# A three-layer graph network on Trainium2: the last 148 nodes handled as an eleventh pair of 74 and 74

## The reference, cut to what matters

```python
h = jnp.maximum(_layernorm(x, axis=-1), 0.0)          # x: 2708 nodes x 512
def _gc(x, adj, W, b):
    return adj @ (x @ W) + b                          # adj: 2708 x 2708, dense float32
h = relu(_gc(h, adj, W1, b1))                         # 512 -> 1024
h = relu(_gc(h, adj, W2, b2))                         # 1024 -> 1024
return x + _gc(h, adj, W3, b3)                        # 1024 -> 512
```

## Time and profile before

| | |
|---|---|
| median of 3 runs | 1592.84 us (1591.72 to 1594.43) |
| the profiled execution, time | 1593.0 us |
| its span, first to last instruction | 1591.2 us |
| PE busy | 1581.1 us, 7674 matmuls |
| DVE, ACT, POOL busy | 872.1, 610.6, 456.3 us |
| PE clock granted | 1.0 throughout |

### The profile page before, as it was taken

One profiled execution on the slowest core, in us unless ns is written; L12 is line 12 of the kernel. 1 busy time (PEld: TensorE's weight loads), 2 busy tenths in 40 slices (PEclk: granted clock), 3 DMA queues, 4 the chain that ended last, 5 costly groups with the idle time before them and its releaser, 6 DMA issues.

```text
span 1591.2 us, 20930 instructions
## 1 busy us (share of the span) xinstructions
PE 1581.1 (99%) x7674; PEld 1360.1 (85%) x7674; DVE 872.1 (55%) x1361; ACT 610.6 (38%) x1076; POOL 456.3 (29%) x417
## 2 busy tenths in 40 slices
PE   9999999999999999999999999999999999999999
PEld 7788889988889898989898989788898888888898
DVE  8973433256553443434564446564565538766856
ACT  5442222234433332323332333443455536454444
POOL 5863544336654000000000015345402214201302
PEclk9999999999999999999999999999999999999999
DMA  6975657644567554545455658884645336887866
GB/s 244 321 225 205 222 179 220 204 138 152 176 220 235 151 153 143 142 118 148 143 169 161 175 186 282 275 298 133 206 120 133 93 93 202 251 249 220 252 191 198
DMA packets 196628, 303.37 MB, mean 191 GB/s; under 512 B 22632, under 2 KB 92608, under 8 KB 196524
## 3 DMA queue, kind: packets, MB, share of 16 engines
q1 hardware_dynamic: 162268, 223.12, 47.1%
q0 software_dynamic: 12224, 43.16, 8.4%
q10 hardware_dynamic: 22032, 35.74, 6.3%
HBM read 219.44 MB, written 82.50 MB: 190 GB/s over the span
## 4 chain that ended last, share of the span: by engine, by line
PE 91%; DVE 5%; DMA 3%; ACT 1%; issue 0%; ACTq 0%; DVEq 0%
PE ps L1731 30%; PE ps L1733 30%; PE ps L1732 30%; DVE slots L1350 1%; PE ps L1824 1%; DVE still L1332 1%; DMA H<-parts 1%; DVE stats L1279 1%; DMA raw<-adjT 0%; DMA raw<-W 0%; DVE ring L1360 0%; DMA raw<-TS 0%; DMA P<-stage_b 0%; DMA raw<-T 0%; ACT slots L1099 0%
## 5 line engine op out<-in xcount | busy, mean ns | idle before, releaser
L1360 DVE TENSOR_TENSOR ring<-raw,ring 128x512 fp32r<-128x512 f32 (+1 forms) x562 | 404.7, 732 | 426.6 <-ACT ring L1131 424.1
L1131 ACT CAST ring<-raw 128x512 fp32r<-128x512 f32 (+1 forms) x562 | 321.3, 577 | 561.9 <-PE ps L1733 464.8
L1731 PE MATMUL ps<-slots,still 128*128 128x512 f32 (+1 forms) x504 | 183.6, 364 | 2.3 <-DVE slots L1350 1.4
L1733 PE MATMUL ps<-slots,still 128*128 128x512 f32 (+1 forms) x504 | 183.1, 363 | 0.0
L1732 PE MATMUL ps<-slots,still 128*128 128x512 f32 (+1 forms) x504 | 183.1, 363 | 0.0
L1733 PE MATMUL ps<-ring,even 128*128 128x512 f32 (+1 forms) x480 | 174.6, 364 | 0.0
L1732 PE MATMUL ps<-ring,even 128*128 128x512 f32 (+1 forms) x480 | 174.6, 364 | 0.0
L1731 PE MATMUL ps<-ring,even 128*128 128x512 f32 (+1 forms) x480 | 174.6, 364 | 0.0
L1587 POOL DMA_DIRECT2D prep<-P x40 | 26.4, 662 | 465.2 <-DMA P<-U 434.4
L1731 PE MATMUL ps<-ring,S 128*128 128x512 f32 (+1 forms) x420 | 153.0, 364 | 0.6 <-DVE ring L1360 0.6
L1733 PE MATMUL ps<-ring,S 128*128 128x512 f32 (+1 forms) x420 | 152.5, 363 | 0.0
(11 more groups left out here) (162 smaller groups left out, 2891.1 us busy)
## 6 DMA issues: line engine op xcount, KB each, us to landing
raw<-TS SPq DMA_DIRECT2D x160, 256.0 KB, 2.9
raw<-adjT SPq DMA_DIRECT2D x138, 256.0 KB, 3.1
raw<-adjT SPq DMA_DIRECT2D x41, 512.0 KB, 4.6
TS<-made SPq DMA_DIRECT2D x20, 1024.0 KB, 6.6
raw<-TS SPq DMA_DIRECT2D x80, 165.0 KB, 2.4
raw<-HS SPq DMA_DIRECT2D x50, 256.0 KB, 2.7
raw<-P SPq DMA_DIRECT2D x45, 256.0 KB, 4.0
raw<-adjT SPq DMA_DIRECT2D x68, 165.0 KB, 2.6
```

The source lines that it names most:

```text
L1131: act.copy(hi, src).then_inc(hi_done, 1)
L1360: dve.tensor_tensor(lo, src, hi.bitcast(F32), ALU.subtract).then_inc(lo_done, 1)
L1731: pe.matmul(out, st_hi, mv_hi, start=start, stop=False)
L1733: return pe.matmul(out, st_lo, mv_hi, start=False, stop=stop)
```

## The change

Block 20 becomes 74 nodes and block 21 the other 74, and they form an eleventh pair (`EXTRA`) that takes part in all seven products. With 74 rows per block, the three products are 222 rows, which are packed in two operands of 128 rows: the first holds lo (74) and the first 54 rows of hi, against hi and hi; the second holds hi (74) and rows 20 to 73 of hi, against lo, zeros and the last 20 rows of hi. `extra_pair` does two matmuls for each column block and every part. The part `None` goes.

For this each group (part and chunk) now loads: the moving rows once into a raw buffer (74 rows and 54 again), cut by ACT alone; a tail (74 rows and 20 rows); and the stationary rows, from new scratch tensors `HX` (pass 2, two tiles once per part) and `HX3` (pass 3, one tile with four transfers in every group). POOL makes the sums of the extra pair and of its adjacency rows (`prep_extra`, stored in `TX`). `extra2` starts at a multiple of 512 bytes, where `left` did not. In w2 the chunks use e(0..3) and e(4..7) by turns for X and Y (`sides`). At the start, the second half of the first adjacency tile is cut before the scale of the second x tile is worked out. In pass 3 all three adds of x that need part 4 follow part 4.

```diff
+REST = 74
+AGAIN = P - REST
+ONCE = REST - AGAIN
+def sides(chunk):
+    return (0, 4) if chunk % 2 == 0 else (4, 0)
...
+def block_width(block):
+    return P if block < 2 * PAIRS else REST
...
-            for part in (0, 1, 2, 3, None, 4, 5, 6):
+            for part in range(7):
...
+                    if i == 0:
+                        tail_step(g, c)
...
+                    if i == 2:
+                        k = p.tile("extra3", False, 4)
+                        n = 7 * c + part
+                        k.part, k.pair = part, n % 3
+                        k.place_freed = ("group", ends[n - 3] if n > 2 else w3_end)
+                        g.extra = k
+                k = p.tile("left", True, 2, low=False)
...
                 elif j.kind == "left":
-                    sp.dma_start(raw[:, r, 0:WIDTH[j.chunk]], adjT[20 * P:21 * P, columns(j.half, j.chunk)]) \
-                        .then_inc(raw_in[r], 16)
+                    w = WIDTH[j.chunk]
+                    sp.dma_start(raw[0:REST, r, 0:w], extra_rows(j.part, j.chunk, 0, REST)).then_inc(raw_in[r], 16)
+                    sp.dma_start(raw[REST:P, r, 0:w], extra_rows(j.part, j.chunk, 0, AGAIN)).then_inc(raw_in[r], 16)
+                elif j.kind == "extra2":
...
+                    sp.dma_start(raw[0:REST, r, :], src).then_inc(raw_in[r], 16)
+                    sp.dma_start(raw[REST:P, r, :], src[again, :]).then_inc(raw_in[r], 16)
+                elif j.kind == "extra3":
...
+                    src = HX3[EXTRA_PLACE[j.part], :, :]
+                    for half in range(2):
+                        cols = slice(half * QUARTER, (half + 1) * QUARTER)
+                        again = slice(0, AGAIN) if half == 0 else slice(ONCE, REST)
+                        sp.dma_start(raw[0:REST, r, cols], src).then_inc(raw_in[r], 16)
+                        sp.dma_start(raw[REST:P, r, cols], src[again, :]).then_inc(raw_in[r], 16)
...
-                    for r in range(3):
-                        sp.dma_start(raw_tail[r * STEP:r * STEP + TAIL, 0, 0:WIDTH[c]],
-                                     adjT[SHORT * P:N, columns(half, c)]).then_inc(tail_in, 16)
+                    sp.dma_start(raw_tail[0:REST, 0, 0:w], extra_rows(a.part, c, 0, REST)).then_inc(tail_in, 16)
+                    sp.dma_start(raw_tail[REST + AGAIN - ONCE:P, 0, 0:w], extra_rows(a.part, c, AGAIN, REST)) \
+                        .then_inc(tail_in, 16)
...
-            def left_over(g, ms, hi, lo, tail, side, started):
+            def extra_pair(g, ms, first, second):
...
                 for m in range(ms):
...
+                    pe.matmul(out, first[:, cols], ring[:, j.slot % RING, 0, 0:w], start=False, stop=False)
+                    pe.matmul(out, second[:, cols], slot_tails[g.tail[0] % 2][:, 0:w], start=False, stop=True) \
+                        .then_inc(group_done, 1)
```

More of the change, by code:

```diff
@@ L504, in go @@
                 b = g.block
[L505 to L517, removed]
+                if EARLY <= pair_of(b) < PAIRS:
                     buf = ("stash", 2 * (b % PAIRS - EARLY) + b // PAIRS)
@@ L574, in pass3 @@
                 g = p.group("pass3", c, part, [2 * pair, 2 * pair + 1])
-                here = list(ORDER) if part is not None else []
-                half = {1: 0, None: 1, 5: 0, 6: 1}.get(part)
-                for t in here:
+                for i, t in enumerate(ORDER):
                     j = p.tile("moving", True)
@@ L616, in store @@
                 p.steps.append(("store", (g, finals, number)))
-            p.later(4 if part == 1 else 2, store)
+            p.later({1: 4, 4: 9}.get(part, 2), store)
     h1_phase(2)
@@ L874, in gcn_kernel, with kept, sums, rows_of @@
         pass3_groups = [g for g in groups if g.phase == "pass3"]
-        kept = [16 * len([t for t in range(PAIRS) if t % PAIR_BUFS == i]) for i in range(PAIR_BUFS)]
+        extra_turn = BLOCKS.index(20) // 2
+        def kept(i, turns):
+            mine = [t for t in range(turns) if t % PAIR_BUFS == i]
+            return 16 * (len(mine) + (extra_turn in mine))
+        def sums(i):
+            return 32 * len([t for t in range(PAIRS + 1) if t % PAIR_BUFS == i])
+        def rows_of(block):
+            return slice(0, block_width(block))
+        def wait_cut(engine, j):
+            if j.low is None:
+                engine.wait_ge(hi_done, j.cut + 1)
+            else:
+                engine.wait_ge(lo_done, j.low)
         @block.sync
@@ L948, in _, with wait_h1, extra_rows @@
             seen = {"p1": 0, "h2": -1}
+            def wait_h1():
+                seen["h1"] = 1
+                for i in range(PAIR_BUFS):
+                    sp.wait_ge(kept_stored[i], kept(i, PAIRS + 1))
+                    sp.wait_ge(sums_stored[i], sums(i))
+            def extra_rows(part, c, first, last):
+                if part in DIRECT:
+                    k, a = DIRECT[part]
+                    start = 2 * PAIRS * P + k * REST
+                    return adjT[start + first:start + last, columns(a, c)]
+                i = {S2: 3, S3: 1, S1: 0, X22: 2}[part]
+                if ("tx", c) not in seen:
+                    seen["tx", c] = 1
+                    for k in (0, 2):
+                        sp.wait_ge(prep_out[k], 16 * (c + 1))
+                return TX[i, first:last, within(c)]
             def load(j):
```

490 lines of the change are left out of this document (249 added, 241 removed).

## The result

The changed kernel takes **1765.68 us** (median; 1759.39 to 1769.43) against 1592.8: 1.108 times as long, 95% interval 1.104 to 1.112. The profiled execution has a span of 1767.3 us against 1591.2, 176.1 more. The timeline of PE, from each stage's first matmul to the next stage's, says where they lie. "Idle" sums the distances of starts beyond the usual 0.227 or 0.150 us where PE stood; "half clock" is the excess of matmuls that follow at 0.427 or 0.275 us. How the slow matmul right behind a gap is counted moves up to 8 us between these two columns in pass 3 and under 1 us elsewhere; their sum doesn't depend on it.

A forecast was written before the change was run, and what follows sets the result against it. PE, busy 1581.1 of 1591.2 us, bounded the kernel before; in the changed one two DMA engines would bind pass 3. 1593.0 - 7.4 (pass 2) - 1.8 (w2) + 106.7 (pass 3) = 1690.5, forecast 1690 us, range 1640 to 1765.

The forecast's parts named there:

- pass 2: Pass 2: fewer left-over matmuls and an aligned operand save 7.4 us, with the added transfers covered.
- w2: w2, third chunk: X and Y by turns remove PE's wait for ACT's copy, -1.8 us, bounds -1.8 and 0.
- pass 3: Pass 3: waits for transfers make it 381 us in place of 274.3, +106.7; ends 342 and 453.
- pass 1, start: Start: cutting the adjacency half before the second x tile's scale changes 0 us, bounds -0.9 and +0.5.
- PE's own work: Matmuls of passes 2 and 3: PE needs 7.4 us less in pass 2 and 2.4 less in pass 3 (271.9).
- The alignment step: Pass 2: the unaligned left-over operand slows its own and neighbouring matmuls; 2.4 of the 7.4 us depend on it.
- Equal shares, 37 rows for an engine: Transfers of 74 rows: split equally, they run on two engines with 37 rows each; the other bound was 5 rows.
- covered, at the slow price just: Pass 2 transfers: 19.8 to 25.8 us in a wide group's 29, 14.5 to 19.6 in a narrow group's 19.2, so no loss.
- The prediction's last rival: The load binds pass 2 as well: pass 3 at 453, 10 us or more in pass 2, over 1765; chance 0.05.
- Pass 3, groups: Pass 3: two-engine load and five raw buffers make a wide group 20.5 us, a narrow one 15.2, total 393.
- its two prices: Pass 3, rate of one DMA engine: 24.2 GB/s fast; slow 18.6 in wide groups, 18.0 in narrow ones.
- Pass 3, lead of nine tiles, -12 us: Start of pass 3: ring and raw buffers begin nine tiles ahead, saving 12 us, 393 to 381.

The follow-up runs named there:

- 72, 73 and 74 rows: Kernel before, each moving tile of pass 3 loaded as 72 and 56, 73 and 55, or 74 and 54 rows: 1600.4, 2524.9, 2002.1 us.
- 64 + 10 rows: Changed kernel, every transfer of 74 rows (loads and stores) issued as one of 64 and one of 10: 1628.6 us, 1.022 times the kernel before.
- the small parts: Kernel before with aligned left-over operand in pass 2 and X, Y by turns in w2 together: 1588.9 us; with the start order alone: 1593.9 us.

## Why the prediction was right, and where it was not

The sign, the cause and the stage were right: 1690 was forecast, 1765.7 measured, 0.7 us past the upper end of the range (1765). That the range nearly holds the total is luck in part. Pass 3, the stage that the range was drawn for, came out at 424 us, between its ends of 342 and 453, and would alone give 1593.0 - 9.2 + 149.9 = 1733.7; the rest are stalls that the sum had at nothing. By its own steps, spans in us:

| term | forecast | measured |
|---|---|---|
| pass 2 | -7.4 | +15.2 |
| w2 | -1.8 | +7.2 |
| pass 3 | +106.7 | +149.9 |
| pass 1, start | 0 | +3.8 |
| sum | +97.5 | +176.1 |

- **PE's own work**: right. Without idle time and half clock pass 2 is 563.3 - 22.5 = 540.8 us, 7.3 less than before, and pass 3 424.2 - 151.6 = 272.6 against 271.9. The alignment step is shown by the aligned operand alone.
- **Equal shares, 37 rows for an engine**: right in what it makes of the time, by 72, 73 and 74 rows. The sign that the prediction took it from, missing landing times, was weak: in the profile after raw<-TS has none either, with 128 rows a tile (2.9 us before).
- **Pass 2, "covered, at the slow price just"**: the step that failed first. At the slow price its own narrow group wasn't covered (19.6 us in 19.2), but the time was lost elsewhere, in wide groups: it set an average load against an average group. The loads come in bursts, and the first waits for a store of 74 rows that SP, in order, can't pass: SP waits for HX<-pair_buf once, 17.0 us, with three moving tiles issued and all others behind it. With 64 + 10 rows this wait is still 11.9 us, so about 5.1 of the 17.0 are due to two engines; most of the rest is the time until ACT issues the store. SP's wait, and the chain behind:

```profile
SPq L1041 <- DMA HX<-pair_buf: 17.0, 1, 17.0
```

```profile
448.50 0.61 DVE extra L1451
449.12 0.23 SPq L1046
449.39 0.61 SPq L1047
450.04 11.69 DMA raw<-adjT
461.75 0.63 ACT ring L1200
```

  A tile of 128 rows lands after 11.7 us, where 3.1 is the median in the kernel before; by the equal shares a sixteenth of its rows is queued behind shares of 37. Four gaps of 1.7 to 7.5 us in the first chunks of parts 0, 1 and 2, with the half-clock matmuls behind them, make nearly all of the 22.5 us. With 64 + 10 rows they are gone. The prediction's last rival asked for 10 us or more in pass 2 and a total over 1765. Both came, but not its mechanism, groups at the engines' limit throughout.
- **w2**: the wait for ACT's copy is gone, here and with the turns alone, but its 1.8 us was the largest of a wait that comes and goes (see the small parts). Not seen: POOL's sums for w2's moving operands end 30.6 us after w2's start where they ended 21.8 us after it, and PE stood 7.2 us for them. POOL's last four rounds of sums, for these operands, take 68.0 us from their first load on, against 59.6 with 64 + 10 rows, and the gap went there too (w2 203.8 us). POOL's own transfers in these rounds all have 128 rows; which other transfer delays them wasn't taken apart.
- **Pass 3, groups**: 20.5 and 15.2 us forecast, 22.0 and 16.6 measured, 14 x 1.5 + 7 x 1.4 = 31 us. The forecast's 456 KB in 22.0 us would be 20.7 GB/s, its 315 KB in 16.6 us 19.0, between its two prices; how much of a group is the engines' rate and how much the five buffers isn't separated. About 12 of the 31 us can have a cause that was in the diff and that no step named: the store of part 4 that waits for POOL with ACT's casts behind it. It costs 12.3 us in the kernel before; in the changed one, with the transfers slow, it was not measured alone. The prediction looked for waits on PE and SP and let ACT pass as "covered".
- **Pass 3, lead of nine tiles, -12 us**: failed. The forecast 381 us, the groups' 31 and these 12 make the 424. PE used three tiles and then stood 6.5 us for the store and load of the first stationary tile, a stall that the mean of 22.0 us holds.
- **Half clock**: not in the sum at all (last section).
- **Start**: 0 forecast, and 0 shown for the order alone. The 3.8 us after are one gap of 3.0 us at 67.6 and seven matmuls at half clock behind it. Pass 1 takes 310.8 to 312.8 us in all kernels built on the one before, the one with the new order (311.7) among them, and 311.3 to 315.7 in those built on the changed one. DVE is busy nearly all the time there in both; why the gap is longer in some isn't settled.

Of the signs, these held: PE x7638, 0.150 us a matmul in narrow groups, w2's wait gone, DMA share and GB/s down (182 and 153; some 190 forecast), ACT's casts ended by transfers. Pass 2 was 15 us longer and not seven shorter, and pass 3 took 424 us and not some 380.

## What to carry to other kernels

Before a tile gets a new height, factor its number of rows: two pieces of 72 and 56 rows cost 9 us here, 74 and 54 cost 411, 73 and 55 cost 932, with the same bytes; issuing the same 74 rows as 64 and a rest of 10 took back 137 of 173 us. When a change moves an instruction that others wait for (here POOL's final adds), look at every in-order engine that waits for it and at what is queued behind that wait, also on engines far below full. And take a stage's load by its bursts, not by its mean.

## What the runs showed of the hardware that I had not expected

- **Half clock after idle time.** PE's timeline at the start of pass 3 (start us, duration, instruction):

```profile
1343.83 0.39 PE L1828 MATMUL ps<-ring,S 128*128 128x512 f32 x1
1350.74 0.76 PE L1826 MATMUL ps<-ring,S 128*128 128x512 f32 x1 [6.53 <-DVE ring L1451]
1351.31 0.63 PE L1827 MATMUL ps<-ring,S 128*128 128x512 f32 x1
1351.73 0.63 PE L1828 MATMUL ps<-ring,S 128*128 128x512 f32 x1
...
1355.41 0.39 PE L1828 MATMUL ps<-ring,S 128*128 128x512 f32 x1
1355.64 0.40 PE L1826 MATMUL ps<-ring,S 128*128 128x512 f32 x1
```

  Behind 6.5 us of idle time the distance of starts is 0.427 us in place of 0.227, the lower of the two levels (1.2 of 2.4 GHz), for 4.7 us. Over the kernel that is some 40 to 45 us of matmul time; the kernel with 73 rows has a granted clock of 0.60 from 1400 to 1800 us, the one with 72 rows 0.98 from 1400 to 1580. Where PE waits for transfers anyway a slower matmul partly fills time that would be idle, so these can't be added to the transfers' price; behind the single gaps of pass 2 its 6.0 us should come on top, which no run separates. The Trainium skill, page "TensorE: Matmul & The Clock Gate", section "What's actually happening", describes the two levels and the fall after idle time; the trace agrees.
- **An issue can hold the issuing engine.** SP's issue, 0.35 us elsewhere, takes 3.00 us with 74 rows and 5.6 with 73, and SP issues nothing else meanwhile: a transfer on two engines delays those that would run on sixteen. That a full queue is the reason fits the two rates above and isn't shown by itself.
- **POOL's transfers are slow with 74 rows too.** Its loads prep<-adjT of 296 KB land after 11.9 us, its stores TX<-prep after 13.0; with the piece of 64 rows, 256 KB, they take 4.9 and 3.1.
- **A pace that depends on a place.** Operands whose offset was no multiple of 512 bytes (64 was kept) cost 3% on their own matmuls and 2% on narrow ones of other operands in the same group.
